# First attention: five wide elementwise operations of GpSimd, each issued as four operations of four heads

## The reference, cut to what matters

```python
q, kv = (x @ w_q), (x @ w_kv)                  # per head, both rotated
lkv = ln(kv window and the one before) * ln_local_g + ln_local_b
pkv = softmax over each segment of 16 tokens of (kv @ w_proj)
gkv = ln(sum over the segment of kv * pkv) * ln_global_g + ln_global_b
attn = softmax([q @ gkv.T, q @ lkv.T], masked) # global and local keys together
out = attn @ [gkv, lkv]
```

## Time and profile before

| | before |
|---|---|
| median of 3 runs, us | 1835.72 (1835.64 to 1851.86) |
| profiled execution, us | 1834.28 |
| its span, us | 1832.5 |
| slots -1 to 8 of the first attention, us from the span's start | about 30 to 765 |
| busy share of the span: TensorE, VectorE, ScalarE, GpSimd | 77%, 67%, 46%, 45% |
| mean granted clock of TensorE, of full speed | 0.85 |

### The profile page before, as it was taken

The page is one execution under the profiler, slowest core; times in us unless marked ns, Lnnn a source line. Parts: engine busy times, 40 slices in busy tenths (PEclk is TensorE's granted clock), DMA queues, the critical chain, the costliest instruction groups (busy, mean ns, idle before and its releaser), DMA issues. The chain is left out here.

```text
span 1832.5 us, 31739 instructions
## 1 busy us (share of the span) xinstructions
PE 1404.4 (77%) x8970; PEld 1111.3 (61%) x8970; DVE 1220.2 (67%) x2837; ACT 843.5 (46%) x2483; POOL 815.8 (45%) x824
## 2 busy tenths in 40 slices
PE   2369686867677869489899898898499889999552
PEld 0236454545454547389889888898166666667452
DVE  4596978787878877274754654744288888887522
ACT  1234343333343335166666666666266555555210
POOL 2563535353535351156566555566354443342103
PEclk7678797868787879599999999999699999988676
DMA  6200000000000000232001100000611111120064
GB/s 210 93 1 3 1 8 1 8 1 8 0 7 1 7 2 7 76 137 86 30 10 73 43 10 11 10 9 9 192 24 31 31 33 33 29 32 9 12 177 113
DMA packets 127183, 72.28 MB, mean 39 GB/s; under 512 B 78296, under 2 KB 118488, under 8 KB 126680
## 3 DMA queue, kind: packets, MB, share of 16 engines
q1 hardware_dynamic: 116664, 60.95, 11.7%
q0 software_dynamic: 3200, 6.56, 1.4%
q10 hardware_dynamic: 7200, 3.41, 0.6%
HBM read 53.26 MB, written 17.12 MB: 38 GB/s over the span
## 5 line engine op out<-in xcount | busy, mean ns | idle before, releaser
L1398 POOL TENSOR_TENSOR hl<-hid,hh 128x256 fp32r<-128x256 f32 x396 | 293.3, 743 | 222.0 <-ACT hh L1375 217.7
L1441 DVE SCALAR_TENSOR_TENSOR hid<-GU,gub,sg 128x256 f32<-128x256 f32 x396 | 190.4, 482 | 195.4 <-ACT sg L1369 126.3
L603 ACT ACTIVATE prob<-S,negmax 128x272 f32<-128x272 f32 (+1 forms) x256 | 107.5, 432 | 343.8 <-DVE negmax L979 343.8
L1269 PE MATMUL GU<-xh,wh 128*128 128x256 f32 x792 | 233.1, 294 | 40.1 <-DVE wl L1417 30.9
L1369 ACT ACTIVATE sg<-GU,gub 128x256 f32<-128x256 f32 x396 | 187.8, 475 | 125.2 <-PE GU L1271 124.5
L1270 PE MATMUL GU<-xl,wh 128*128 128x256 f32 x792 | 225.4, 285 | 0.0
L1271 PE MATMUL GU<-xh,wl 128*128 128x256 f32 x792 | 225.2, 284 | 0.0
L1805 ACT ACTIVATE prob<-S,negmax 128x256 f32<-128x256 f32 x256 | 118.9, 469 | 158.2 <-DVE negmax L2190 152.3
L1269 PEld LDWEIGHTS GU<-xh,wh 128*128 128x128 f32 x792 | 152.0, 192 | 49.9 <-issue 27.1
L1375 ACT CAST hh<-hid 128x256 fp32r<-128x256 f32 x396 | 158.1, 399 | 27.0 <-DVE hid L1441 25.8
L485 PE MATMUL PT<-const,prob 128*128 128x128 f32 x384 | 81.9, 339 | 97.4 <-DVE prob L974 97.3
(11 more groups left out here) (289 smaller groups left out, 3375.0 us busy)
## 6 DMA issues: line engine op xcount, KB each, us to landing
raw<-in_expert_w SPq DMA_DIRECT2D x4, 2688.0 KB, 12.5
modb<-mod_d SPq DMA_DIRECT2D x2, 2688.0 KB, 15.2
list<-zero SPq DMA_DIRECT2D x5, 1024.0 KB, 9.6
raw<-in_expert_w SPq DMA_DIRECT2D x4, 1152.0 KB, 6.6
wa<-in_w SPq DMA_DIRECT2D x16, 256.0 KB, 3.3
wb<-in_w SPq DMA_DIRECT2D x16, 256.0 KB, 3.8
kpad<-rel_d SPq DMA_DIRECT2D x1, 3072.0 KB, 13.4
qkv_d<-qkvT SPq DMA_DIRECT2D x24, 128.0 KB, 4.3
```

What stands on the lines that cost most here:

```text
L1269: pe.matmul(out, lhs[0], rhs[0], start=start, stop=False, skip_group_check=True)
L1398: pool.tensor_tensor(hl[:, b], hid[:, b], hh[:, b].bitcast(F32), ALU.subtract).then_inc(hid_lo, 1)
L1441: dve.scalar_tensor_tensor(out=hid[:, c % BUFS], in0=GU[c % BUFS][:, TT:2 * TT], scalar=gub[:, UP, e * CH0 + c:e * CH0 + c + 1], in1=sg[:, ...
```

## The change

Each 128x1024 operation of GpSimd in the first attention (L1080, L1091, L1095, L1100, L1107) becomes four of 128x256, four heads each, issued one after the other with no wait between them; the semaphore is raised by the fourth. The operations of 128x512 (L1073), VectorE's program, its scalings (L974) among it, and every wait stay as they are. In `normalise` 6 operations become 24 (4 become 16 in slot -1), in `weigh` 2 become 8, in each call of `logit_products` 1 becomes 4.

```diff
+            PIECES = [slice(k, k + H0 // 4) for k in range(0, H0, H0 // 4)]
+
             def per_head(a):
-                return a[:, None, :].broadcast_to([P, H0, DH0])
+                return a[:, None, :].broadcast_to([P, H0 // 4, DH0])
...
-                pool.tensor_tensor(heads_of(wk[:, t, :]), heads_of(kvr[:, t, :]), per_head(wproj[:]), ALU.mult).then_inc(lg_mul, 1)
+                for g in PIECES:
+                    i = pool.tensor_tensor(heads_of(wk[:, t, :])[:, g], heads_of(kvr[:, t, :])[:, g], per_head(wproj[:]), ALU.mult)
+                i.then_inc(lg_mul, 1)
...
                 for t in range(TILES):
-                    pool.tensor_tensor(heads_of(V[:, bp, t, :]), heads_of(kvc[:, t, :]),
-                                       krs[:, t, :, None].broadcast_to([P, H0, DH0]), ALU.mult).then_inc(kv_norm, 1)
+                    for g in PIECES:
+                        i = pool.tensor_tensor(heads_of(V[:, bp, t, :])[:, g], heads_of(kvc[:, t, :])[:, g],
+                                               krs[:, t, g, None].broadcast_to([P, H0 // 4, DH0]), ALU.mult)
+                    i.then_inc(kv_norm, 1)
                 for t in range(TILES):
                     pool.wait_ge(kv_norm, 6 * b + 1 + t)
-                    pool.tensor_tensor(heads_of(V[:, bp, t, :]), heads_of(V[:, bp, t, :]), per_head(lng[:, 0, :]),
-                                       ALU.mult).then_inc(kv_norm, 1)
+                    for g in PIECES:
+                        i = pool.tensor_tensor(heads_of(V[:, bp, t, :])[:, g], heads_of(V[:, bp, t, :])[:, g], per_head(lng[:, 0, :]), ALU.mult)
+                    i.then_inc(kv_norm, 1)
...
```

More of the change, by code:

```diff
@@ L1099, in normalise @@
                         pool.wait_ge(kv_norm, 6 * b + 3 + t)
-                        pool.tensor_tensor(heads_of(V[:, bp, t, :]), heads_of(V[:, bp, t, :]), per_head(lng[:, 1, :]),
-                                           ALU.add).then_inc(kv_norm, 1)
+                        for g in PIECES:
+                            i = pool.tensor_tensor(heads_of(V[:, bp, t, :])[:, g], heads_of(V[:, bp, t, :])[:, g], per_head(lng[:, 1, :]), ALU.add)
+                        i.then_inc(kv_norm, 1)
             def weigh(slot, b):
@@ L1106, in weigh @@
                     pool.wait_ge(lg_red, 2 * b + t + 1)
-                    pool.tensor_tensor(heads_of(wk[:, t, :]), heads_of(kvr[:, t, :]),
-                                       pk[:, t, :, None].broadcast_to([P, H0, DH0]), ALU.mult).then_inc(wk_done, 1)
+                    for g in PIECES:
+                        i = pool.tensor_tensor(heads_of(wk[:, t, :])[:, g], heads_of(kvr[:, t, :])[:, g],
+                                               pk[:, t, g, None].broadcast_to([P, H0 // 4, DH0]), ALU.mult)
+                    i.then_inc(wk_done, 1)
             def normalise_pooled(slot, b):
```

## The result

| | before | changed |
|---|---|---|
| median, us (lowest to highest of 20 runs each) | 1839.85 (1832.91 to 1851.86) | 1848.83 (1838.97 to 1860.17) |
| profiled execution, its span, us | 1834.28, 1832.5 | 1851.54, 1849.7 |
| mean granted clock of TensorE | 0.85 | 0.84 |
| end of the first attention (start of L1038), us | 758.5 | 770.95 |

The changed kernel takes 1.0044 times as long, 95% interval 1.0023 to 1.0064: 8 us more, where 1.2 us less was forecast. That is within the 1% called no change and inside the range of 1818 to 1852, but the interval leaves 1 out: a small loss, on the side opposite to the forecast. Before and after were run side by side for this ratio, so it needs no correction for the 1835.72 from which the forecast set out. Runs more than 1.5% above the fastest one of their kernel are left out of every ratio, and no profile of such a run is used.

The account below looks back on a forecast made before the run. No engine full; TensorE waits most for VectorE's scalings, each held by GpSimd's wide operations. Slots 1 to 5 -5.0, slot 0 +2.6, slot -1 +2.8, slot 6 -1.6: -1.2 us, median 1834.5, range 1818 to 1852.

Parts of the forecast that it names:

- The price of a piece: GpSimd's 128x256 pieces spaced 0.58 or 0.69 us; each wide operation cut in four grows by 0.46 us.
- The new wait: VectorE before L738, slots 1 to 5: waits for GpSimd's rs from about 389 to 397.0 in slot 3's times.
- Slot -1: Four wide operations grow by 1.8 us, VectorE's wait with them; L759 waits 1.0 more for L1073: together +2.8 us.
- Slot 6: No rs here, VectorE runs free; pooled sums 2.0 us earlier as the weighing ends sooner; -1.6 with logit products.
- (a): Normalisation and weighing: pieces cost 0.83 us each, GpSimd's train delays rs and L738; +32 us, about 1866; chance 0.12.
- (b): GpSimd's trains: a piece costs a quarter of a wide operation; -4.5 us in 7 slots, about 1804; chance 0.09.
- Slots 1 to 5, at the normalisation: rs 3.1 us later, but TensorE's transposes start at 402.6 instead of 404.02, pooled sums earlier: -1.4 us a slot.
- Slot 0: VectorE already waits for rs, so GpSimd's 3.1 us fall wholly on the path; +2.6 us after gains and costs behind.
- rival (c): A train of pieces keeps VectorE out until its end, priced at the normalisation's scalings; +24 us, about 1859; chance 0.04.
- From there on nothing changes: Slot 7 has none of the cut operations; from there to the kernel's end the forecast was no change.
- the logit term: Slots 1 to 5, logit products: L767 gains about 0.8 us twice, scalings and L857 give back 0.6 each; together +0.4.
- Rival (d): Shorter stops leave TensorE at its higher clock level behind them: -1.0 us a slot, about 1827; chance 0.15.

Follow-up runs that it names:

- experiment 7: Idle matmuls ahead of TensorE's wait for scaled probabilities: kernel before with 26, 18, 12: ratios 1.0194, 1.0025, 0.9985; changed kernel with 22, 14: 1.0035, 1.0009.
- again: The changed kernel run and profiled once more with no edit: 1847.09 us against 1841.34 for the kernel before, ratio 1.0015.
- experiment 3: Kernel before with only one place in pieces: normalisation 1847.26 us (1.003), weighing 1825.83 us (0.9935), logit products 1833.49 us (0.9936).

## Why the prediction was wrong

What it said of GpSimd and VectorE was right, in mechanism and mostly in size; what it said of TensorE was not. The total hangs on three terms.

**Right.** *The price of a piece.* Forecast 0.58 and 0.69 us, and an end 15.7 + 0.6 = 16.3 us after the start. Measured in slot 3: 24 pieces in 15.97 us (388.20 to rs at 404.17), against 13.2 before. *The scalings*: four pieces, 2.9 us; measured 2.38. *The new wait*: 8 us before L738 (389 to 397.0); measured 8.77, 8.0 in slot 1. L738 "starts 1.1 us later": 22.4 against 21.5 us into the slot, 0.9. The stop of TensorE moved from the fifth to the sixth head pair. *Slot -1*: L821's wait for the four grown operations went from 8.24 to 9.94 us (forecast +1.8), but the 1.0 us more of the logit products isn't there: +1.5 in all instead of +2.8. *Slot 6*: -2.0 at the pooled sums, measured -1.9 in A. The range held the measured time, but a range of 34 us about a sum of -1.2 says little; the sign was wrong. Rivals (a) and (b), with pieces of 0.83 us and a quarter, are out by these rows (groups of GpSimd, changed kernel, 98 to 700):

```profile
L1102 POOL TENSOR_TENSOR V<-V,lng 128x256 f32<-128x256 f32 x56 | 40.0, 748 | 0.0
...
L1096 POOL TENSOR_TENSOR V<-kvc,krs 128x256 f32<-128x256 f32 x56 | 34.3, 647 | 1.3 <-POOL krs L1088 1.1
```

**The step that failed: "Slots 1 to 5, at the normalisation", -1.4 each.** It rests on "TensorE before was not waiting for them at all: its queue ... reached these transposes at 404.02". That is true of slot 3, on which all of it was read, and the start of the pooled sums did come 1.5 us sooner there (30.6 us into the slot, from 32.1). It is not true of all five. Slot 2 of the kernel before, TensorE, whose L1084 is at 285.4:

```profile
312.15 0.87 PE L501 MATMUL O<-pT,V 128*64 128x256 f32 x8
...
313.17 0.55 PE L485 MATMUL PT<-const,prob 128*128 128x128 f32 x3
...
315.30 0.66 PE L446 MATMUL A<-const,V 128*128 128x128 f32 x4 [1.04 <-DVE rl L896]
```

The same operation in slot 3:

```profile
402.54 1.55 PE L501 MATMUL O<-pT,V 128*64 128x256 f32 x8
```

TensorE's stop at the fifth head pair is nearly as long in slot 2 (8.47 us, 8.71 in slot 3), and VectorE's scalings start 26.7 us into the slot in both. So the stop was not what made the queue late in slot 3; TensorE's level was: the granted clock is 0.50 from 400 to 405 us in slot 3 and 1.00 from 311 to 316 in slot 2. In slots 1 and 2 TensorE is back at its higher level (0.55 us for three transposes, 0.90 in slot 3), has caught up and waits for VectorE's L896. VectorE reaches L896 29.2, 29.7 and 29.7 us into slots 1 to 3 before, and 29.3, 29.7 and 29.4 after: the change moves it by 0.35 us at most. L446 starts 29.9 us into slot 2. In slot 3 it started 31.4 us in, and after the change 29.6: the change brings slot 3 to where slots 1 and 2 already were, and there it has nothing to win.

What the change then costs in slots 0 to 5 is TensorE at its lower level behind the new stop: in slot 3 L446 takes 1.11 us and L429 1.71, where L429 took 1.09. In slots 0 to 5 these two groups take 6.3 us more in sum (second profile of the changed kernel against the one before), and experiment 7 gets about 1 us of it back in each of slots 2, 3 and 5. So slot 3 keeps 0.9 of its 1.5 us, and slots 1 and 2 lose 1.5 and 0.9. Over slots 1 to 5 A changed by +0.5 us a slot (again: +0.1) instead of -1.4. Which slots of the kernel before had the lower level is partly luck of its one profile: with the logit products alone in pieces, slot 3 has the same VectorE rows and A is 33.8. The views that would have told it were there: A by slot, 33.3 and 33.8 against 35.4, and the releaser of L446.

**Slot 0: +2.6 forecast, +5.2 measured.** L738 starts 2.6 us later into the slot (3.1 forecast). The rest has two parts. One is rival (c), given 0.04 and priced at the normalisation (where it doesn't happen: the scalings got in after one piece each), turning up at the weighing (slot 0; VectorE, then GpSimd):

```profile
140.74 4.88 DVE L738 TENSOR_SCALAR h<-xt,mv,rs 128x128 f32<-128x128 f32 x2 [9.97 <-POOL rs L1148]
```

```profile
140.68 4.61 POOL L1116 TENSOR_TENSOR wk<-kvr,pk 128x256 f32<-128x256 f32 x8
```

L738 waits for all eight pieces, 4.88 us, where 1.3 had been forecast; what stands behind it then meets no piece, so that the transposes start 3.7 us later into the slot, 1.1 more than forecast. The other part is TensorE's level again: before, the six transposes, L446 and L429 ran at the higher one, and now L446 takes 1.06 us instead of 0.60 and L429 1.66 instead of 1.09. These, with the transposes, are the other 1.5 us. With the logit products alone in pieces GpSimd and VectorE run as before in this slot up to L1025, TensorE stays at its lower level, and A is 2.1 us longer: that level needs no late rs. In slot 0 L738 is held off in both profiles of the changed kernel, in slot 4 in one of them (4.80 against 1.11 us, and A 36.9 against 34.6). Where GpSimd's rs and the first piece of its next train follow one another with nothing between, VectorE, released by that same rs, can be held off for the whole train. The Trainium skill (SBUF — State Buffer, Who interferes with whom) says that whoever issues first has the pair of ports for its whole instruction; the trace agrees for one wide operation at a time, but here the holder was eight instructions, 4.61 us.

**"From there on nothing changes", and B.** Forecast 0 behind slot 6 and +0.4 a slot from the logit products. The measured sign of the logit term alone is the other way, -0.65 us (experiment 3). B as a whole became 4.5 us longer (again: 3.4), 2.8 of it behind slot 6, where no operation was changed. The changed kernel has 88.6 to 89.1 us there in three profiles, with rs late or early; with one of the three places cut alone it is 83.6 to 85.7, before 85.9. What does it is open, and with it about 40% of the loss at the stage's end.

**Rival (d)**, TensorE's clock turning with a shorter stop, came true in reverse: the stop didn't shorten, it moved, right ahead of the pooled sums. In A this is shown slot by slot (above, and experiment 7); how much of the total is the clock's isn't settled.

The sum by the measured parts: A +7.6 (again: +5.3) and B +4.5 (again: +3.4), 12 and 9 us at the stage's end, against the 8 us of the timed runs.

## What to carry to other kernels

Cutting one engine's operations so that another can get in between is paid at the end of the cut train: ask first what is queued behind the train and who waits for it (here a 0.7 us operation, whose move ahead of the train turned +0.15 to 0.44% into -1.2%), and leave that train wide: cutting the other two, with the short operation early, gave -1.7%. Before pricing a repeated stage from one of its repetitions, tabulate the same stretch in all of them and see whether the same wait ends last: a gain read in the slowest repetition may only bring it level with the rest. And look at the level of TensorE's clock in each: a stop that moves to just ahead of a critical group of matmuls makes that group slower.

## What the runs showed of the hardware that was not expected

- A train of GpSimd operations with nothing between can hold VectorE's first operation off for all of it: 4.88 us at eight pieces of 0.58 us (slot 0), though the same operation gets in after one piece in slots 1, 2, 3 and 5 (1.11 to 1.21 us). VectorE starts 0.06 us after the train in slots 0 (held off) and 1 (not), 0.14 in slot 4 (held off) and 0.15 in slot 3 (not): what decides isn't clear.
- Behind two stops of nearly the same length (8.47 and 8.71 us), with VectorE's operations at the same distances, TensorE was back at its higher level in one slot and still at its lower in the next (kernel before, slots 2 and 3: granted clock 1.00 and 0.50 in the stretch from 25.6 to 30.6 us into the slot, A 33.8 and 35.4 us).
- GpSimd loses little to VectorE: the weighing takes 5.08 us with L738, L741, L743 and scalings beside it in slot 3, and 4.61 in slot 0, where VectorE is held off. The share of 0.4 from the earlier trace rows was rather high: it put 0.6 us on the 15.7 of the normalisation, where the measured 15.97 leaves 0.3.
- Cut in four, the two weighing operations take 4.61 us instead of 3.76, 0.43 us more for each; in eight, an operation of the normalisation takes another 0.6 us (6.12 against 4.90 us for two of L1096).
- A power on 128x32 takes GpSimd 5.43 us and doesn't hold VectorE's scalings off: four of them beside it in the kernel before take their undisturbed 1.04 us, at 376.24 beside L1084, which starts at 374.4.
